# Second attention layer continued in the first layer's block and weight ring: first 256 nodes' maxima and shift ahead of the rest, low row parts on GpSimd

## What is computed

```
def _gat_layer(x, src, dst, W, a_src, a_dst, bias, concat):
    h = (x @ W).reshape(N, H, C)
    al_s = jnp.einsum('nhc,hc->nh', h, a_src)
    al_d = jnp.einsum('nhc,hc->nh', h, a_dst)
    e = jax.nn.leaky_relu(al_s[src] + al_d[dst], NEG_SLOPE)
    m = jax.ops.segment_max(e, dst, num_segments=N)
    ex = jnp.exp(e - m[dst])
    denom = jax.ops.segment_sum(ex, dst, num_segments=N)
    alpha = ex / (denom[dst] + 1e-16)
    out = jax.ops.segment_sum(h[src] * alpha[:, :, None], dst, num_segments=N)
h = elu(_gat_layer(h, ..., W1, 4 heads of 512, concat=True))
x = x + _gat_layer(h, ..., W2, 1 head of 768, concat=False)      # attention block
x = x + gcn(relu(gcn(relu(layernorm(x)), G1)), G2)               # convolution block
```

## Time and profile before

| what | value |
|---|---|
| runs | 1186.42, 1191.17, 1191.92 us |
| the profiled execution: its own time | 1188.23 us |
| its span in the trace | 1186.5 us |
| mean granted TensorE clock | 0.986 of full |
| busy: PE, PEld, DVE, ACT, POOL | 94%, 88%, 71%, 43%, 3% |
| first layer's last product starts | 772.78 us |
| second layer's first sum starts | 797.42 us |

### The profile page before, as it was taken

One profiled execution on the slowest core, in us unless ns is written; L12 is line 12 of the kernel. 1 busy time (PEld: TensorE's weight loads), 2 busy tenths in 40 slices (PEclk: granted clock), 3 DMA queues, 4 the chain that ended last, 5 costly groups with the idle time before them and its releaser, 6 DMA issues. The chain is left out here.

```text
span 1186.5 us, 17506 instructions
## 1 busy us (share of the span) xinstructions
PE 1114.7 (94%) x7124; PEld 1045.2 (88%) x7124; DVE 836.6 (71%) x1390; ACT 513.0 (43%) x1052; POOL 30.4 (3%) x40
## 2 busy tenths in 40 slices
PE   5999999999999999999999999739999899999998
PEld 5878886789989998999999999729999899889998
DVE  7998896899768886788768778679856623341263
ACT  4232322375547654556547654155445613431120
POOL 4200001020000000000000000000000000000000
PEclk9999999989999999999999999969999999999999
DMA  6133130021011100201020100013002300000321
GB/s 221 66 113 116 40 122 18 1 63 54 1 51 40 54 1 1 89 16 40 1 69 22 54 1 1 1 56 115 28 27 68 116 1 1 27 14 1 131 75 56
DMA packets 27618, 58.44 MB, mean 49 GB/s; under 512 B 3492, under 2 KB 6152, under 8 KB 27536
## 3 DMA queue, kind: packets, MB, share of 16 engines
q1 hardware_dynamic: 27344, 56.96, 14.5%
q10 hardware_dynamic: 192, 0.32, 0.1%
HBM read 41.73 MB, written 15.54 MB: 48 GB/s over the span
## 5 line engine op out<-in xcount | busy, mean ns | idle before, releaser
L1330 PE MATMUL banks<-hs,ring_hi 128*128 128x258 f32 (+1 forms) x1600 | 299.4, 288 | 2.8 <-DVE z L997 2.8
L1330 PEld LDWEIGHTS banks<-hs,ring_hi 128*128 128x128 f32 (+1 forms) x1600 | 247.9, 188 | 4.2 <-DVE z L997 3.0
L1330 PE MATMUL banks<-hs,ring_lo 128*128 128x258 f32 (+1 forms) x800 | 227.0, 284 | 0.0
L248 ACT ACTIVATE e<-banks,al 128x256 f32<-128x256 f32 (+1 forms) x500 | 193.9, 491 | 22.4 <-PE banks L233 22.4
L1330 PEld LDWEIGHTS banks<-hs,ring_lo 128*128 128x128 f32 (+1 forms) x800 | 150.9, 189 | 0.0
L256 ACT ACTIVATE ring_hi<-pf 128x512 fp32r<-128x512 f32 (+1 forms) x125 | 81.6, 653 | 159.8 <-DVE pf L267 156.6
L1358 PE MATMUL banks<-w_hi,oT_hi 128*128 128x384 f32 (+1 forms) x320 | 109.5, 342 | 12.7 <-DVE rows L1025 6.9
L265 DVE TENSOR_TENSOR e<-e 128x512 f32<-128x512 f32 (+1 forms) x125 | 84.5, 676 | 36.6 <-ACT e L248 36.4
L1358 PE MATMUL banks<-w_lo,oT_hi 128*128 128x384 f32 (+1 forms) x320 | 109.0, 341 | 0.0
L1358 PE MATMUL banks<-w_hi,oT_lo 128*128 128x384 f32 (+1 forms) x320 | 108.9, 340 | 0.0
L1204 PE MATMUL banks<-w_hi,xT_hi 128*128 128x512 f32 x240 | 97.4, 406 | 0.5 <-DVE w_lo L781 0.5
(11 more groups left out here) (262 smaller groups left out, 2109.7 us busy)
## 6 DMA issues: line engine op xcount, KB each, us to landing
h_scratch<-stage SPq DMA_DIRECT2D x30, 256.0 KB, 2.0
hs<-h_scratch SPq DMA_DIRECT2D x30, 256.0 KB, 2.9
w_st<-in_L_gnn_W SPq DMA_DIRECT2D x4, 1536.0 KB, 7.4
w_st<-in_L_gnn_W SPq DMA_DIRECT2D x16, 384.0 KB, 3.5
gw_st<-in_L_gnn_W SPq DMA_DIRECT2D x12, 384.0 KB, 3.8
xr<-in_x SPq DMA_DIRECT2D x9, 384.0 KB, 10.1
rows<-in_x SPq DMA_DIRECT2D x9, 384.0 KB, 3.2
x_scratch<-rows SPq DMA_DIRECT2D x9, 384.0 KB
```

The source lines that it names most:

```text
L248: last = nc.scalar.activation(self.e[:, local % 2, a, i, 0:n], self.p_shift[:, a, 0:n], ACT.Exp, bias=scores[a][:, g * G + i:g * G + i + 1])
L1330: last = nc.tensor.matmul(p_a[0:m, dt, half, 0:HH], wt.ring[a][:, s // G, s % G, dt * P:dt * P + m], hs[:, s, b, half * HH:(half + 1) * HH ...
```

## The change

The two later blocks are gone: one block holds everything, and each engine's list goes on into the second layer. Part by part:

1. `last_shift` is dissolved into the first layer's lists, and the second layer uses the first's ring, `e` and `pf`, with the counters going on (SECOND = 20 stands where 0 stood).
2. `mask` is stored rotated by two tiles (`mask_slot`), so that source tiles 8 and 9 lie where `hs2` doesn't; `hs2` is written over the mask of tiles 0 to 7 and over the first layer's rows. The mask is made by two instructions instead of one.
3. In the last head the source scores come singly between `add_products`; the destination scores of tiles 6 to 9 come later, in the first chunk of the second layer.
4. Tiles 8 and 9 go into `top` first for columns 0 to 255 alone; two transposes, a reduction of 128x2 and `shift_parts` of two tiles give the first chunk's shifts. The other 1024 columns, eight transposes, their reductions and shifts are done beside the first chunk's sums (`turn_rest`, `turn_shift`, `spread_rest`, behind source tiles 1, 5 and 6).
5. `products` waits for `elu_lo` per tile, and `turn_out(19, 0)` and `(19, 1)` come before and behind the last piece of `products(18)`.
6. ACT's high row parts come in two lots, four before the last `elu_hi` and six behind. The ten low row parts are GpSimd's.
7. The first chunk starts with the terms that need only high weights, for the first two source tiles, before `lo_ready`.
8. The broadcast for chunk 1 comes behind source tile 6 instead of 1. PSUM banks, the largest degree's turn and the load of the input rows (now also behind the scores) move along.

The diff, without changes of indentation and cut to its core:

```diff
+def mask_slot(t):
+    return (t + NDT) % T
...
+            def second_lo(t):
+                pool_.wait_ge(hi2_done, t + 1)
+                nc.gpsimd.tensor_tensor(hs2[1][:, t, 0:D], rows[:, t, :], hs2[0][:, t, 0:D].bitcast(fp32),
+                                        ALU.subtract).then_inc(lo2_done, 1)
+
+            for t in range(6):
+                second_lo(t)
+            half.ones(pool_)
+            for t in range(6, T):
+                second_lo(t)
+            half.gpsimd(pool_)
...
+            def second_hi(t):
+                act.wait_ge(wt.used, (SECOND + 1) * NG)
+                act.wait_ge(top_step, tops_until((1, 2, 3, 4, 6, 7, 7, 7, 7, 7)[t]))
+                act.wait_ge(g_out, final_row(t))
+                nc.scalar.activation(hs2[0][:, t, 0:D], rows[:, t, :], ACT.Copy).then_inc(hi2_done, 1)
+
+            for t in range(4):
+                second_hi(t)
             for dt in range(NDT):
-                elu_hi(HEADS * NC - 1, dt)
+                elu_hi(SECOND - 1, dt)
+            for t in range(4, T):
+                second_hi(t)
+            second = al[:, :, 0], al02[:, :, 0]
+            for g in range(NG):
+                wt.exps(nc, act, second, SECOND, 0, g)
+                if g >= 1:
+                    wt.hi(nc, act, SECOND, 0, g - 1)
+            wt.hi(nc, act, SECOND, 0, NG - 1)
+            half.scalar(act)
...
-            nc.vector.tensor_scalar(mask[:, :, :], counts[:, :, :], 0.0, FAR, ALU.is_equal, ALU.mult).then_inc(mask_ready, 1)
+            for of_mask, of_counts in ((slice(0, NDT), slice(T - NDT, T)), (slice(NDT, T), slice(0, T - NDT))):
+                nc.vector.tensor_scalar(mask[:, of_mask, :], counts[:, of_counts, :], 0.0, FAR, ALU.is_equal, ALU.mult).then_inc(mask_ready, 1)
...
+            second_top(1)
+            elu_lo(end - 1, 0)
+            second_top(2)
+            second_top(3)
+            elu_lo(end - 1, 1)
+            second_top(4)
+            second_top(5)
             normalize(end)
             add_products(end - 1, range(2))
             elu_out(end)
-            add_products(end - 1, range(2, NB))
-            for dt in range(NDT):
-                elu_lo(end, dt)
-            score_rows(chunk_tiles(NC - 2))
-            final_tiles = chunk_tiles(NC - 1)
-            for i in range(NB):
-
-                second_tops(range(TOPS + i * (final_tiles[0] - TOPS) // NB, TOPS + (i + 1) * (final_tiles[0] - TOPS) // NB))
-                add_products(end, (i,))
-                if i % 2:
-                    score_rows(final_tiles[i // 2:i // 2 + 1])
+            score_row(6, 0)
+            add_products(end - 1, range(2, 3))
+            elu_lo(end, 0)
+            add_products(end - 1, range(3, NB))
+            score_row(7, 0)
+            elu_lo(end, 1)
+            second_top(6)
+            add_products(end, range(1))
+            second_top(7)
+            add_products(end, range(1, 2))
+            score_row(8, 0)
+            slope(slice(0, NDT), HEADS)
+            add_products(end, range(2, 3))
+            second_top(8, FIRST_COLS)
+            add_products(end, range(3, NB))
+            score_row(9, 0)
+            dve.wait_ge(scored, scored_at[9, 0])
+            dve.wait_ge(top_step, n_top[0])
+            nc.vector.scalar_tensor_tensor(out=top[:, FIRST_COLS], in0=mask[:, mask_slot(9), FIRST_COLS], scalar=al[:, 9, 0:1],
+                                           in1=top[:, FIRST_COLS], op0=ALU.add, op1=ALU.max).then_inc(top_ready, 1)
+            slope(slice(0, T), 0)
+            blocks = 3 * (HEADS - 1) + 1
+            dve.wait_ge(top_t, 2 * HEADS)
+            nc.vector.tensor_reduce(mem.amax[:, 0:NDT], p_first, AX.X, ALU.max).then_inc(reduced, 1)
+            shift_parts(nc, chain, mem, 0, lambda: dve.wait_ge(reduced, blocks + 1), shift_ready, slice(0, NDT))
+            dve.wait_ge(shift_t, HEADS + 1)
+            nc.vector.tensor_copy(shiftT[:, 0, :], p_shift_first).then_inc(shift_out, 1)
+            second_top(8, REST_COLS)
             dve.wait_ge(top_step, n_top[0])
-            dve.wait_ge(scored, 2 * T)
-            nc.vector.tensor_scalar(al02[:, :, 0:HEADS + 1], al[:, :, 0:HEADS + 1], SLOPE, None, ALU.mult).then_inc(scored, 1)
-            dve.wait_ge(scored, 2 * T + 1)
+            nc.vector.scalar_tensor_tensor(out=top[:, REST_COLS], in0=mask[:, mask_slot(9), REST_COLS], scalar=al[:, 9, 0:1],
+                                           in1=top[:, REST_COLS], op0=ALU.add, op1=ALU.max).then_inc(top_ready, 1)
+            wt.weigh(nc, dve, counts, SECOND, 0, 0)
+            score_row(6, 1)
+            wt.lo(nc, dve, SECOND, 0, 0)
+            wt.weigh(nc, dve, counts, SECOND, 0, 1)
+            score_row(7, 1)
+            wt.lo(nc, dve, SECOND, 0, 1)
+            dve.wait_ge(top_t, 2 * HEADS + 1)
+            for b in range(2):
+                nc.vector.tensor_reduce(mem.amax[:, NDT + 4 * b:NDT + 4 * b + 4],
+                                        p_g[b].rearrange("p (k c) -> p k c", c=P), AX.X, ALU.max).then_inc(reduced, 1)
+            wt.weigh(nc, dve, counts, SECOND, 0, 2)
+            score_row(8, 1)
+            wt.lo(nc, dve, SECOND, 0, 2)
+            score_row(9, 1)
+            slope(slice(NDT, T), HEADS)
+            dve.wait_ge(scored, scored_at["all"])
+            shift_parts(nc, chain, mem, 0, lambda: dve.wait_ge(reduced, blocks + 3), shift_ready, slice(NDT, T))
+            wt.weigh(nc, dve, counts, SECOND, 0, 3)
+            wt.lo(nc, dve, SECOND, 0, 3)
+            dve.wait_ge(shift_t, HEADS + 2)
+            nc.vector.tensor_copy(shiftT[:, 2, :], p_shift_rest).then_inc(shift_out, 1)
+            wt.weigh(nc, dve, counts, SECOND, 0, 4)
+            wt.lo(nc, dve, SECOND, 0, 4)
+            half.vector(dve)
...
+            products(SECOND - 2, range(3))
+            turn_out(SECOND - 1, 0)
+            products(SECOND - 2, range(3, NB))
+            turn_out(SECOND - 1, 1)
+            products(SECOND - 1)
...
+            pe.wait_ge(top_ready, HEADS + 1)
+            for t in range(NDT):
+                last = nc.tensor.transpose(p_first[:, t, :], top[:, t * P:(t + 1) * P], ident[:, :])
+            last.then_inc(top_t, 1)
+            turn_shift(HEADS, p_shift_first)
+            pe.wait_ge(shift_out, HEADS + 1)
+            wt.broadcast(nc, pe, pick, shiftT[:, 0, :], SECOND, 0)
...
+            half.tensor(pe, {1: turn_rest, 5: lambda: turn_shift(HEADS + 1, p_shift_rest), 6: spread_rest})
...
+            sp.wait_ge(scored, 2 * 6 if t < 6 else 2 * T + 2)
...
+        pe.wait_ge(wt.hi_ready, SECOND * NG + 1)
+        for s in range(G):
+            pe.wait_ge(lo_done, s + 1)
+            for dt in range(NDT):
+                pair(0, s, dt, TERMS[0:2])
...
+                if s == G - 1 and 1 <= c < NC - 1:
+                    wt.broadcast(nc, pe, pick, shiftT[:, 2, :], SECOND + c + 1, c + 1)
+                if c == 0 and s in first_chunk:
+                    first_chunk[s]()
```

More of the change, by code:

```diff
@@ L1092, in _ @@
                             (lambda: take_peaks(h, 0), lambda: take_peaks(h, 1), lambda: keep_shift(h))[g - 1]()
+                    scoring = final and c >= 2
+                    row = (c - 2) * NDT
                     if last is not None:
@@ L1343, in sums, with products @@
                         turn_out(q - 1, TURNS.index(s))
-            def products(q):
+            def products(q, which=range(NB)):
                 h, c = q // NC, q % NC
-                pe.wait_ge(olo_done, (q + 1) * NDT)
                 if c == 0:
@@ new lines, in spread_roots @@
+        def spread_roots(j):
+            pe.wait_ge(turn_out, 1)
+            if j:
+                pe.wait_ge(wide_out, j)
+            t0, t1 = WIDE[j]
+            for t in range(t0, t1):
+                last = nc.tensor.matmul(p_wide[:, (t - t0) * P:(t - t0 + 1) * P], pick[:, t:t + 1].to_broadcast([4 * T, P]),
+                                        shiftT[:, 1, :], start=True, stop=True)
+            last.then_inc(wide_ready, 1)
+        beside = {(1, 1): turn_greatest, (1, 7): turn_roots, (2, 7): lambda: spread_roots(0), (3, 7): lambda: spread_roots(1),
+                  (4, 3): lambda: spread_roots(2)}
@@ new lines, in pair @@
+        def pair(c, s, dt, terms):
+            t = c * NDT + dt
+            m = rows_of(t)
+            for half in range(2):
+                for j, (a, b) in terms:
+                    last = nc.tensor.matmul(p_a(t)[0:m, half, 0:AH], wt.ring[a][:, s // G, s % G, dt * P:dt * P + m],
+                                            hs[b][:, s, half * AH:(half + 1) * AH],
+                                            start=s == 0 and j == 0, stop=s == T - 1 and j == 2)
+            return last
+        TERMS = list(enumerate(((0, 0), (0, 1), (1, 0))))
@@ new lines, in spread, with spread_lows @@
+        def spread(d, half, s, a):
+            m, k = rows_of(d), rows_of(s)
+            last = nc.tensor.matmul(p_q(d)[0:m, half, :], d_hi[0:k, d % 2, s, 0:m], z[a][0:k, s, half * HALF:(half + 1) * HALF],
```

(12 more changed lines are left out.)

1054 lines of the change are left out of this document (502 added, 552 removed).

## The result

| | before | change |
|---|---|---|
| median, range (runs) | 1188.78, 1186.15 to 1193.9 (20) | 1183.98, 1179.85 to 1188.3 (20) |
| ratio to before, 95% interval | | 0.995, 0.9938 to 0.9961 |
| profiled execution, its span | 1188.23, 1186.5 us | 1184.0, 1181.9 us |

The change saves 4.8 us in the medians, 4.6 to 7.4 by the interval of the ratio. Forecast was 7.4 against the profiled execution, 1181 us, in a range of 1170 to 1188; the time of 1183.98 lies in it. The ratio of 0.995 stands on the edge of what the forecast called faster, over 0.5%.

A forecast was written before the change was run, and what follows sets the result against it. TensorE, busy 94% of the span, was taken as the bound, so only its gaps and slow stretches could be won. Terms -7.1 - 14.7 + 2.3 + 3.3 + 8.8 = -7.4 us from 1188.23 gave 1181 us, range 1170 to 1188.

The forecast's parts named there:

- A: First layer's tail: TensorE's four stops for DVE, 7.15 us in all, go away; -7.1 us.
- E: Low row parts on GpSimd hold up DVE operations with two SBUF operands, seven of ten rows at 1.25 us; +8.8 us.
- no stop over 1 us would show: Sign for the first layer's tail: TensorE has no stop over 1 us between 742 us and its last product.
- B: Gap from the first layer's last product to the second layer's first sum: 9.6 us instead of 24.3; -14.7 us.
- 10 to 16: Sign for the hand-over between layers: last product to first sum takes 10 to 16 us.
- C: Second layer's first chunk gets longer by eight transposes, a turn and waits on `lo`; +2.3 us.
- D: Second chunk is late after its later broadcast: a stop of 3.8 us instead of 0.5 at its second tile; +3.3 us.
- the 1 us for waits on `lo`: First chunk of the second layer: sums wait 1 us for low weights because DVE has some 17 us of work.
- the port is hardly contested: Rival: GpSimd's rows slip into DVE's waits and one-operand work, costing 0 to 1 us; time 1172, chance 0.18.
- the slower case, a long row: Rival: long GpSimd rows hold the port in the tail; at 5.1 us per row they cost 22.9 us; 1195 us, chance 0.07.
- every row stretches an operation on the path: Rival: all ten GpSimd rows stretch DVE operations on the path, costing 12.5 us; time 1184.5, chance 0.13.
- DVE as the bound of the first two chunks: Rival: the wait moves from the gap into the second layer's sums, adding 4 to 5 us; 1185.5 us, chance 0.10.

The follow-up runs named there:

- short rows: The changed kernel with GpSimd subtracting only 4 of 768 columns of each low row part, sums reading the high rows instead; 1174.03 us, ratio 0.9876.
- the run with both moves: The changed kernel with eight transposes ahead of the first sums, second turn and broadcast one tile earlier, `finish` of two tiles ahead of the fourth weight group; 1178.7 us.
- late rows: The changed kernel with GpSimd beginning its ten low row parts only when DVE has copied the first chunk's shifts; 1185.49 us, ratio 0.9951.
- the first experiment: The changed kernel with GpSimd subtracting only 4 of 768 columns of each low row part, sums reading the high rows; 1174.03 us, ratio 0.9876.

## Why the prediction was right, point by point

**A, tail stalls: -7.1 forecast, -4.8 measured; E hid in it.** Without the rows the last matmul comes 8.0 us nearer, so the argument (one or two passes of `top` ahead of each `elu_lo`, a product piece over each turn) held and was a little low; the four stops of before explain 7.15 of it, the rest stays open. I had said "I take all 7.1" and that no stop over 1 us would show; two of 1.4 us show, the first because `elu_out` took 2.93 us beside rows, for 1.28 without, the second because the add stood behind a pass of `top` of 2.63.

**B, last product to first sum: -14.7 forecast, -13.8 measured.** The short rows give 10.9 us from start to start, 10.5 from the end of the last product, where the chain summed to 9.6. My sign "10 to 16" failed for the change itself, where it is 17.2 from start to start and 16.9 from the end: E was mostly in the gap, and I had not put it there.

**C and D, first chunk and the stop behind it: +5.6 forecast, +4.5 measured.** The first chunk's sums took 25.8 us instead of 24.2 (+1.6, forecast 2.3), the stop 2.92 instead of 0.39 (+2.5, forecast 3.3). The other 0.3 lies in the second chunk, where the largest degree's turn (L1961) now stands: the prediction had put that move at nothing. Of C, the matmuls taken in were sized rightly (1.3 forecast; 1.04 for the transposes and 0.41 for the turn), and the 1 us for waits on `lo` was wrong: the sums never waited for one in the change. In D the chain was right, four groups of weights and then `finish`: `finish` moved ahead of the fourth group cut the stop from 2.92 to 0.94 us. What I had not seen is DVE's wait of 3.95 us for eight transposes that TensorE's list holds back behind two source tiles; without it the second chunk's sums were done 1.7 us sooner, though the stop stayed at 3.11:

```profile
794.61 1.04 PE L1498 MATMUL banks<-ident,top 128*128 128x128 f32 x8
804.23 0.41 PE L1388 MATMUL banks<-ident,parts 128*40 128x128 f32 x2
822.22 0.38 PE L1961 MATMUL banks<-ident,dmax 128*1 128x128 f32 x2
```

```profile
795.68 1.29 DVE L1242 TENSOR_REDUCE amax<-banks 128x4 f32<-128x512 f32 x2 [3.95 <-PE banks L1498]
```

That the order of the lists is what makes D, and that it can be shortened by moves alone, the run with both moves shows (3.8 us).

**E, GpSimd beside DVE: +8.8 forecast, +9.6 measured.** The size is right, its parts are not quite. A row took 1.79 us at the shortest (estimate 1.96), and a held operation lost 0.7 to 1.7 us, nine of them 11.2 us in sum, where I had taken seven at 1.25. Of the 11.2 us, 9.6 reached the first sum. The earlier trace rows had shown the hold in three instructions, and that was enough.

The exclusive lock of the Trainium skill (SBUF — State Buffer, "SBUF: two separate sides") stands behind this term, and the traces agree with it: beside the late rows each operation of 0.69 us with two SBUF operands takes 2.17 to 2.32, held by most of a row's 1.79, and in the change the adds with one operand from PSUM keep their 0.54 us. The Trainium skill (SBUF — State Buffer, "Who interferes with whom") says that a `tensor_scalar` of DVE can take the pair too; the slopes, with a single input, took 1.82 and 1.77 us. The Trainium skill (Perfetto Trace Analysis, "Optimizing Scalar/DVE Operations") warns that offloading between these two engines "might not help"; here it cost 9.6 us up to the first sum to spare DVE ten parts of 0.87.

**The sum.** -8.0 - 13.8 + 9.6 + 4.5 = -7.7 us at the end of the second chunk, forecast -7.4. That the two agree to 0.3 us is in part luck: the terms were off by 0.9 (A), 0.9 (B), 0.8 (E) and 1.1 us (C and D), and the errors cancel. The medians show 4.8 and the ratios 0.5%, some 6 us. A term that the forecast lacked lies outside the span: 1.7 us before and in the two kernels with the parts on DVE, 2.0 to 2.25 in every execution on record of the kernels with instructions for the parts on GpSimd, which takes some 0.35 us off the gain. Of the two traces of the change one stands at -7.7 and the other at -6.4, by the clock after the new stop. I had costed D in full-clock time alone: the stop is a chance for the clock to fall, which it did not do in the trace of before, with 0.39 us. That the rest of the difference is clock elsewhere fits the spread of 7.8 and 8.5 us over the runs of either kernel, but is not shown.

**The rivals.** That the port is hardly contested fell with the first experiment, and the slower case, a long row, with a shortest row of 1.79 us and a longest of 3.16. That every row stretches an operation on the path (+12.5) is too much, though nearer in its count (nine held) than my seven: rows one to six were partly swallowed by the tail's waits. DVE as the bound of the first two chunks is true in part: its list sets D; with the parts between the first chunk's weights TensorE waits for low weights too (2.1 us).

## What to carry to other kernels

In this kernel, work moved from DVE to GpSimd was free only while DVE stood still or worked from PSUM; price it as rows met times most of a row's own time (1.4 to 1.6 of 1.79 us where DVE is dense), on the engine that you meant to relieve. Before moving work off a busy engine, look for its own waits: with the parts back on DVE, three of them in its waits, and with the transposes, the second turn and `finish` moved forward, the kernel is 12 us faster than the change by the medians and 13 by the ratios, with all ten parts still DVE's. A new stop of some 3 us of TensorE should carry the price of a fall of the clock with it, as a chance; here the fall cost 1.6 us.

## What I had not expected of the hardware

- The length of a DVE operation doesn't matter for the hold: a product of 128x2 values waited out a row as a pass over 128x1280 did (1.82 us for 0.17; 2.63 for 1.54).
- With two streams of such instructions the engines alternated, in the run with late rows: ten rows in 23.83 us, nine DVE operations held in turn by 1.4 to 1.6 us and a tenth by 0.4, while a row takes 1.79 us at the shortest.
- After a stop of 1.8 to 4.2 us at the second chunk the granted clock fell in five of nine profiled executions (25.0 to 26.1 us from `rden` to `rden`) and stayed in four (23.4), even for the same program. With stops under 1 us it stayed in both other traces of changed kernels.
